# Memory layer of a hybrid model: recalls by head pairs on block-diagonal memories, values subtracted on GpSimd, recalled values turned by transposes

## The reference, cut to what matters

```python
def step(carry, inp):
    mem, z = carry
    q_s, k_s, v_s, qn_s, kn_s = inp
    scores = jnp.einsum('bhnd,bhmd->bhnm', q_s, k_s) * SCALE
    sdpa = jnp.einsum('bhnm,bhmd->bhnd', softmax(where(mask, scores, -inf)), v_s)
    sq, sk = elu1(qn_s), elu1(kn_s)
    num, den = sq @ mem, (sq @ z)[..., None]
    out = beta * num / (den + 1e-06) + (1.0 - beta) * sdpa
    prev_v = (sk @ mem) / (sk @ z)[..., None]
    mem = mem + sk.T @ (v_s - prev_v)
    z = z + sk.sum(axis=2)
    return (mem, z), out
```

## Time and profile before

| what | value |
|---|---|
| median of the runs | 2560.41 us |
| span of the profiled execution | 2623.8 us |
| instructions in it | 79243 |
| TensorE matmul busy | 2176.9 us (83%) |
| VectorE busy | 1700.0 us (65%) |
| ScalarE busy | 1437.8 us (55%) |
| GpSimd busy | 1106.7 us (42%) |
| memory layer, first instruction to the last addition to x | 1729 to 2450 us |

### The profile page before, as it was taken

One profiled execution on the slowest core, in us unless ns is written; L12 is line 12 of the kernel. 1 busy time (PEld: TensorE's weight loads), 2 busy tenths in 40 slices (PEclk: granted clock), 3 DMA queues, 4 the chain that ended last, 5 costly groups with the idle time before them and its releaser, 6 DMA issues. The chain is left out here.

```text
span 2623.8 us, 79243 instructions
## 1 busy us (share of the span) xinstructions
PE 2176.9 (83%) x30448; PEld 1549.2 (59%) x30448; DVE 1700.0 (65%) x5819; ACT 1437.8 (55%) x3704; POOL 1106.7 (42%) x1076
## 2 busy tenths in 40 slices
PE   6499948589964889899999977948999999999696
PEld 3288845379862233333334336937778777787396
DVE  6722247642336778787878833358999989899522
ACT  5455544355552256455455555537777767776353
POOL 2066644146654120120200004547777777776164
PEclk7699979789986799998989888969999999999798
DMA  4011120011125121111111000121111111111013
GB/s 133 33 42 43 43 85 2 33 32 44 43 93 163 55 58 31 38 39 31 35 46 35 5 33 29 41 85 54 54 53 56 52 53 55 52 56 52 35 42 92
DMA packets 76025, 134.96 MB, mean 51 GB/s; under 512 B 17225, under 2 KB 32264, under 8 KB 73224
## 3 DMA queue, kind: packets, MB, share of 16 engines
q1 hardware_dynamic: 62080, 102.07, 12.6%
q0 software_dynamic: 13568, 27.81, 3.7%
q10 hardware_dynamic: 8, 0.00, 0.0%
HBM read 65.19 MB, written 32.79 MB: 37 GB/s over the span
## 5 line engine op out<-in xcount | busy, mean ns | idle before, releaser
L1544 ACT ACTIVATE ca_pt<-ca_ps 128x512 f32<-128x512 f32 (+3 forms) x768 | 341.1, 491 | 322.3 <-PE ca_ps L1649 137.2
L734 PE MATMUL ffn_ps<-ffn_xst,ffn_up_w 128*128 128x128 f32 x3392 | 420.8, 278 | 0.2 <-issue 0.2
L734 PEld LDWEIGHTS ffn_ps<-ffn_xst,ffn_up_w 128*128 128x128 f32 x3392 | 402.9, 195 | 1.2 <-issue 1.2
L857 DVE TENSOR_TENSOR ffn_hid<-ffn_sg,ffn_ps 128x512 f32<-128x512 f32 x212 | 145.8, 688 | 359.2 <-PE ffn_ps L734 110.9
L576 POOL DMA_INDIRECT ffn_xs<-ffn_x,ffn_token_at x212 | 205.2, 968 | 301.5 <-DVE ffn_token_at L840 165.5
L581 POOL DMA_INDIRECT ffn_y<-ffn_ys,ffn_result_at x212 | 208.8, 985 | 139.2 <-DVE ffn_ys L863 82.3
L1645 PE MATMUL ca_ps<-ca_stacks 75*128 75x512 bf16 (+3 forms) x768 | 245.2, 342 | 18.3 <-ACT ca_pt L1544 10.7
L1777 DVE TENSOR_REDUCE ca_m_far<-ca_ps 128x1 f32<-128x128 f32 (+5 forms) x384 | 236.7, 616 | 30.3 <-PE ca_ps L1623 27.9
L643 ACT ACTIVATE ffn_sg<-ffn_ps 128x512 f32<-128x512 f32 x212 | 125.7, 593 | 233.6 <-remote 182.3
L1623 PE MATMUL ca_ps<-ca_stacks 72*128 72x512 bf16 (+3 forms) x768 | 223.4, 356 | 34.1 <-DVE ca_m_near L1778 21.9
L1778 DVE CUSTOM_DVE_ANT_0 ca_spill<-ca_ps,ca_bias_q 128x256 f32<-128x256 f32 (+1 forms) x512 | 201.1, 397 | 10.9 <-PE ca_ps L1623 10.9
(11 more groups left out here) (340 smaller groups left out, 4742.0 us busy)
## 6 DMA issues: line engine op xcount, KB each, us to landing
im_mates<-im_t SPq DMA_DIRECT2D x256, 128.0 KB
ffn_got<-ffn_y SPq DMA_DIRECT2D x48, 256.0 KB, 5.8
ca_stacks<-scratch_q_piece SPq DMA_DIRECT2D x16, 576.0 KB
ca_stacks<-scratch_k_piece SPq DMA_DIRECT2D x48, 192.0 KB
ffn_x<-ffn_xn SPq DMA_DIRECT2D x32, 256.0 KB, 2.0
w_w<-in_L_ffn_experts_w_dram SPq DMA_DIRECT2D x2, 2048.0 KB, 12.0
ffn_xs<-ffn_x,ffn_token_at POOLq DMA_INDIRECT x212
ffn_y<-ffn_ys,ffn_result_at POOLq DMA_INDIRECT x212
```

What stands on the lines that cost most here:

```text
L734: last = nc.tensor.matmul(ps[:, bank, j * P:j * P + P], up_w[:, n % WS, first + j * P:first + j * P + P], xst[:, n % 2, :], start=True, st ...
L1544: nc.scalar.activation(pt[:, i % 8, lo - c0:hi - c0], ps[:, tile_bank(i), lo - c0:hi - c0], ACT.Exp, scale=SCALE).then_inc(p_ready, 1)
```

## The change

1. A second copy of the memories, `mem_by`, holds for each of the two heads of a pair a block of 65 columns, with that head's memory on its own half of the partitions and zeros on the other. SyncE fills it: at slot k, behind the two DMAs for `mates`, it waits for `mem_ready` of step k - 4 and sends the two halves of that step's memory, two DMAs of 64 partitions with 520 float32 each.
2. `prev` and `num` run over pairs: 8 float32 matmuls each, of a 128x32 stationary piece on 130 columns of `mem_by`. All of `prev` is in bank 0 and all of `num` in bank 1. `prev` waits for those DMAs (`placed`) in place of `mem_ready`.
3. VectorE forms the recalled value times the reciprocal of all four heads by one instruction (`known`), and GpSimd subtracts the values (`surprise`), between `spread` and `rotate` of its slot.
4. The recalled values are turned by `transpose` in place of the matmul with the identity.
5. GpSimd sets `mem_by` ahead of the loops, 4160 columns on 128 partitions and twice 32 columns on 64, and TensorE and VectorE wait for that too.

```diff
+        mem_by = s.sb("mem_by", [P, NQ, 2, BATCH, PB, E1])
...
-        prev_view, num_view = (both_banks(c, PB * E1).rearrange("p e (k d) -> p e k d", k=PB) for c in (PR, NU))
+        prev_view, num_view = (ps[:, bank, 0:QH * E1].rearrange("p (h d) -> p h d", d=E1) for bank in range(2))
...
                     for odd in range(2):
                         sp.dma_start(mates[1 - odd:P:2, k % 2, :], t2[odd:P:2, k % 2, :]).then_inc(mates_ready[k % 2], 16)
+                    if 0 <= k - 4 < N - NQ:
+                        j = k - 4
+                        sp.wait_ge(S["mem_ready"], j + 1)
+                        for e in range(2):
+                            half = slice(D * e, D * e + D)
+                            sp.dma_start(mem_by[half, j % NQ, e], mem[half, j % NQ]).then_inc(placed[j % NQ], 16)
...
                 pool.wait_ge(S["made"], 13)
+                nc.gpsimd.memset(mem_by[:], 0.0).then_inc(S["made"], 1)
+                pool.wait_ge(S["made"], 14)
+                for e in range(2):
+                    nc.gpsimd.memset(mem_by[D * e:D * e + D, :, e, :, :, D:E1], 1.0e-6).then_inc(S["made"], 1)
+                pool.wait_ge(S["made"], 16)
...
+                def surprise(j):
+                    pool.wait_ge(S["known"], j + 1)
+                    pool.wait_ge(S["lifted"], j + 1)
+                    new = uu[:, j % 2, :, 0:D]
+                    nc.gpsimd.tensor_tensor(new, new, values_of(j), ALU.subtract).then_inc(S["u_ready"], 1)
...
                     if 0 <= k - 3 < N:
                         spread(k - 3)
+                    if 0 <= k - 3 < LEARNED:
+                        surprise(k - 3)
                     if k < N:
                         rotate(k)
...
+                def for_pairs(fn):
+                    for blk in range(PB):
+                        for b in range(BATCH):
+                            last = fn(blk, b, slice(SEG * b, SEG * b + SEG))
+                    return last
...
-                        nc.tensor.matmul(ps[:, UP + n, OT:OT + P], m1[:, j % 2, 2 * n:2 * n + 2, :].rearrange("p h d -> p (h d)"), g.ident[:], start=True, stop=False, skip_group_check=True)
+                        nc.tensor.transpose(ps[:, UP + n, OT:OT + P], m1[:, j % 2, 2 * n:2 * n + 2, :].rearrange("p h d -> p (h d)"), g.ident[:])
...
-                        pe.wait_ge(S["mem_ready"], j - NQ + 1)
-                    for_heads(lambda half, bank, blk, b, tok: nc.tensor.matmul(ps[tok, bank, PR + blk * E1:PR + blk * E1 + E1], el[half, r, PB + blk, tok], mem[half, q, b, blk, :],
+                        pe.wait_ge(placed[q], 32 * (j // NQ))
+                    for_pairs(lambda blk, b, tok: nc.tensor.matmul(ps[tok, 0, blk * 2 * E1:blk * 2 * E1 + 2 * E1], el[:, r, PB + blk, tok], mem_by[:, q, :, b, blk, :],
...
-                    for h in range(QH):
-                        e, n = h // PB, h % PB
-                        last = nc.vector.scalar_tensor_tensor(uu[:, r, h, 0:D], prev_view[:, e, n, 0:D], rd[:, h:h + 1], values_of(j)[:, 2 * n + e, :], ALU.mult, ALU.subtract)
-                    last.then_inc(S["u_ready"], 1)
+                    nc.vector.tensor_tensor(uu[:, r, :, 0:D], prev_view[:, :, 0:D], bl(rd[:], D), ALU.mult).then_inc(S["known"], 1)
```

More of the change, by code:

```diff
@@ L1856, in memory_layer @@
     E1 = D + 1
-    PR, NU, SC = 0, PB * E1, 2 * PB * E1
+    SC = 2 * PB * E1
     UP, OT = 4, 192
@@ L1899, in memory_layer @@
                  "ab_used", "below_ready", "er_ready", "below_exp", "el_ready", "rope_ready", "lift_ready", "lifted", "scored", "recalled", "s1_ready", "rd_ready", "nm_ready",
-                 "u_ready", "den_ready", "dn_ready", "m1_ready", "p_ready", "share_ready", "own_gated", "rsum_ready", "pn_ready", "pt_ready", "pte_ready",
-                 "upd_ready", "mem_ready", "weighed", "ot_copied", "out_ready", "x_ready", "stats")
+                 "known", "u_ready", "den_ready", "dn_ready", "m1_ready", "p_ready", "share_ready", "own_gated", "rsum_ready", "pn_ready", "pt_ready", "pte_ready",
+                 "upd_ready", "mem_ready", "placed_a", "placed_b", "placed_c", "placed_d", "weighed", "ot_copied", "out_ready", "x_ready", "stats")
         S = {n: s.sem(n) for n in names}
         mates_ready = (S["mates_even"], S["mates_odd"])
+        placed = (S["placed_a"], S["placed_b"], S["placed_c"], S["placed_d"])
         def both_banks(first, width):
@@ L2113, in prev @@
                     if j >= NQ:
-                        pe.wait_ge(S["mem_ready"], j - NQ + 1)
-                    for_heads(lambda half, bank, blk, b, tok: nc.tensor.matmul(ps[tok, bank, PR + blk * E1:PR + blk * E1 + E1], el[half, r, PB + blk, tok], mem[half, q, b, blk, :],
-                                                                               start=True, stop=True, skip_group_check=True))
+                        pe.wait_ge(placed[q], 32 * (j // NQ))
+                    for_pairs(lambda blk, b, tok: nc.tensor.matmul(ps[tok, 0, blk * 2 * E1:blk * 2 * E1 + 2 * E1], el[:, r, PB + blk, tok], mem_by[:, q, :, b, blk, :],
+                                                                   start=True, stop=True, skip_group_check=True))
                 def num(j):
                     q, r = j % NQ, j % 3
-                    for_heads(lambda half, bank, blk, b, tok: nc.tensor.matmul(ps[tok, bank, NU + blk * E1:NU + blk * E1 + E1], el[half, r, blk, tok], mem[half, q, b, blk, :],
-                                                                               start=True, stop=True, skip_group_check=True)).then_inc(S["recalled"], 1)
+                    for_pairs(lambda blk, b, tok: nc.tensor.matmul(ps[tok, 1, blk * 2 * E1:blk * 2 * E1 + 2 * E1], el[:, r, blk, tok], mem_by[:, q, :, b, blk, :],
+                                                                   start=True, stop=True, skip_group_check=True)).then_inc(S["recalled"], 1)
                 def lift_values(k):
@@ L2167, in learn @@
                                 tok = slice(SEG * b, SEG * b + SEG)
-                                last = nc.tensor.matmul(b_up[half, b, blk * E1:blk * E1 + E1], keys[tok, blk, half], uu[tok, r, PB * parity + blk, :],
+                                last = nc.tensor.matmul(b_up[half, b, blk * E1:blk * E1 + E1], keys[tok, blk, half], uu[tok, r, 2 * blk + parity, :],
                                                         start=True, stop=True, skip_group_check=True)
@@ L2176, in lift_keys @@
                     last.then_inc(S["lift_ready"], 1)
-                pe.wait_ge(S["made"], 13)
+                pe.wait_ge(S["made"], 16)
                 for c in range(2 * BATCH):
@@ L2217, in _ @@
                 dve.wait_ge(S["g_ready"], 1)
-                dve.wait_ge(S["made"], 13)
+                dve.wait_ge(S["made"], 16)
                 nc.vector.tensor_scalar_add(gate[:, 1:3, :], gate[:, 1:3, :], 1.0).then_inc(S["setup"], 1)
@@ L2260, in recall @@
                                                    ALU.mult, ALU.add).then_inc(S["s1_ready"], 1)
-                    nc.vector.reciprocal(rd[:].rearrange("p (e k) -> p e k", e=2), prev_view[:, :, :, D]).then_inc(S["rd_ready"], 1)
+                    nc.vector.reciprocal(rd[:], prev_view[:, :, D]).then_inc(S["rd_ready"], 1)
                     dve.wait_ge(S["s1_ready"], j + 1)
@@ L2264, in recall @@
                     dve.wait_ge(S["rd_ready"], j + 1)
-                    nc.vector.scalar_tensor_tensor(dn[:].rearrange("p (e k) -> p e k", e=2), num_view[:, :, :, D], 1.0e-6,
-                                                   gate[:, 1, q * QH:q * QH + QH].rearrange("p (k e) -> p e k", e=2), ALU.add, ALU.mult).then_inc(S["den_ready"], 1)
-                    dve.wait_ge(S["lifted"], j + 1)
+                    nc.vector.scalar_tensor_tensor(dn[:], num_view[:, :, D], 1.0e-6, gate[:, 1, q * QH:q * QH + QH], ALU.add, ALU.mult).then_inc(S["den_ready"], 1)
                     if 2 <= j < LEARNED:
                         dve.wait_ge(S["upd_ready"], j - 1)
-                    for h in range(QH):
-                        e, n = h // PB, h % PB
-                        last = nc.vector.scalar_tensor_tensor(uu[:, r, h, 0:D], prev_view[:, e, n, 0:D], rd[:, h:h + 1], values_of(j)[:, 2 * n + e, :], ALU.mult, ALU.subtract)
-                    last.then_inc(S["u_ready"], 1)
+                    nc.vector.tensor_tensor(uu[:, r, :, 0:D], prev_view[:, :, 0:D], bl(rd[:], D), ALU.mult).then_inc(S["known"], 1)
                     dve.wait_ge(S["den_ready"], j + 1)
@@ L2278, in recall @@
                         dve.wait_ge(S["weighed"], j - 1)
-                    nc.vector.tensor_tensor(sorted_heads(m1[:, r]), num_view[:, :, :, 0:D], over(dn[:], D), ALU.mult).then_inc(S["m1_ready"], 1)
+                    nc.vector.tensor_tensor(m1[:, r], num_view[:, :, 0:D], bl(dn[:], D), ALU.mult).then_inc(S["m1_ready"], 1)
                 def add(p):
```

## The result

The changed kernel takes 2567.14 us (median of 20 runs) against 2559.05; the ratio is 1.0037, 95% interval 1.0023 to 1.0052. It is slower, by 8.1 us, a little less than half of the 17.6 us forecast. The profiled execution spans 2564.0 us, but that of before 2623.8, so the two are compared by layer and not by span.

The account below looks back on a forecast made before the run. A circle of waits between VectorE and TensorE was taken to bound each slot; a new one of 5.26 us plus 0.15 against 5.31 gave +12.4 us, memset +4.2, rounded up to +17.6: 2578 us, range 2548 to 2610.

Parts of the forecast that it names:

- a new circle through `spread`, the subtraction and `learn`: From remember over turn_p, spread, GpSimd's subtraction and learn back to remember: 5.26 us a slot, replacing the old circle's 5.11.
- Disturbances: Late partner DMAs and features holding up L2248 add 0.15 us a slot, with 0.07 and 0.35 as bounds.
- The end: Last two tiles, where TensorE has twice the output products and no room: total rounded up from +16.6 to +17.6 us.
- The circle's length: Sum of the waits and operations around the new circle: 5.26 us, between 5.20 and 5.33, with 0.61 for the subtraction.
- Recalls, transposes, placing: In each slot: recalls by pairs take 0.59 us, two transposes save 0.17 us on TensorE, placing DMAs cost nothing.
- Ahead of the loops: GpSimd's memset of 4160 columns and two small ones, all on the path since TensorE waits for them: +4.2 us.
- Rival 2: At L2155, learn meets its operand in time and TensorE's slot of 5.0 us decides: faster, 2539 us, chance 0.14.
- Rivals 3 and 4: 3: later DMAs, 0.35 us a slot, 2602 us, chance 0.12; 4: column groups do not overlap, +370 us, chance 0.02.
- Rival 1: Same circle, but late partner DMAs cost 0.07 us a slot, covered by GpSimd's new work: 2567 us, chance 0.34.

Follow-up runs that it names:

- `light_behind`: Kernel before with one-instruction multiplication on VectorE, GpSimd's subtraction behind spread and transposes, recalls single, no second copy; ratio 1.0068 to the kernel before.
- `vector_subtracts`: Changed kernel with the subtraction back on VectorE in four instructions; ratio 1.0008 to the kernel before.
- `doubled`: Changed kernel with one more GpSimd operation of 128x256 between spread and the subtraction, result unused; 2695.64 us against 2601.27 of the kernel before on that chip.
- `sub_first`: Changed kernel with GpSimd's subtraction ahead of spread instead of behind it; ratio 0.9942 to the kernel before.
- `light`: Kernel before with one-instruction multiplication on VectorE, GpSimd's subtraction ahead of spread and transposes, recalls single, no second copy; ratio 0.9935 to the kernel before.

## Why the prediction was right in sign and too large in size

- *Sign and mechanism.* Right: the main forecast, slower by a new circle through `spread`, the subtraction and `learn`. Moving it away, lengthening it and rebuilding it without the pairs all moved the time as the circle says.
- *The sum.* Forecast were +12.4 us in the slots, +4.2 ahead of the loops and +1.0 at the end; the traces have +8.5, +3.5 and -4.1. Two terms failed: the disturbances of a slot and the end.
- *Disturbances, the first step that failed.* I took 0.15 us a slot on top of the circle; it is 0.08, about 8 us less in all. Two smaller errors hid most of this in the slots' sum: the circle is 0.05 us longer than forecast, about 6 us, and the mean slot of before, which I read as 5.31 from the middle of the layer, is 5.33 over all of it, about 2 us. `light_behind` shows that 0.15 would have been near for single recalls (0.18). GpSimd waited for partner DMAs in 52 slots before, 50.5 us. With single recalls and the subtraction's cover, in `light_behind`, it is 19 slots and 17.6 us. What I did not see is that the kernels with recalls by pairs are disturbed less besides: 16 slots and 10.2 us in the changed kernel, and 27.2 us without the cover, in `vector_subtracts`. Why is open.
- *The end, the second step that failed.* I added 1 us for the last tiles, since TensorE has twice the output products there; the trace has -4.1 us. I had read only the middle of the layer, where `learn` bounds. At the end it does not exist, and the shorter recall and a clock that did not fall come out as a gain. Of the three parts of the sum this one missed by most, 5.1 us, and a part of it may be chance, as said above.
- *The circle's length.* 5.26 us forecast, 5.30 to 5.31 measured. The term at fault is the subtraction: 0.61 by L1989, 0.68 in fact. L1989 reads broadcast operands; `doubled`'s added operation of the same size, which does not, took 0.73. Half of `spread`'s 1.27 us would have said 0.64.
- *Recalls, transposes, placing.* Recalls by pairs 0.58 (0.59). The two transposes took 0.38 us against 0.61, a little better than L2175 promised. Placing nothing, as forecast.
- *Ahead of the loops.* +4.2 forecast, +4.0 to TensorE's start, +3.5 to the first sines.
- *Rivals.* Rival 2 named the right place, L2155: in `sub_first`, where the way from `turn_p` to `learn` no longer holds the subtraction, TensorE's own slot decides with 5.07 us (5.08 by the forecast's sum). Rivals 3 and 4 fell. Rival 1, 2567 us from disturbances of 0.07, has the measured time and the measured size of the disturbances, although I gave the forecast more. That its time is met to the microsecond is in part luck: its slot of 5.33 us is 0.06 too short, and the end that it leaves out gives most of that back.

## What to carry to other kernels

Work that is moved to an idle engine lands in a queue. Ask what stands in front of it there, and how much earlier its reader used to get its operand. Here 0.68 us of work behind `spread` made a clean slot 5.30 us long instead of 5.11; with the same work ahead of `spread` it is 5.07. Read the first and last turns of a loop too, since another chain can bound them.

## What was not expected

- TensorE, padded to the old number of instructions while the doubled DMA traffic runs, stood still for up to 1.98 us (PEld at L2144) in the loops, with no wait in the profile. The kernel before, with as many instructions and without that traffic, showed at most 1.1 us at L2115, but `light`, also without it, once showed 1.90 us (PEld at L2123). So the traffic is not shown to be the cause, and what TensorE lacks there is open.
- A memset on GpSimd, which reads nothing, took VectorE's normalisation from 2.14 to 4.10 us. The first of the eight operations lasted 2.50 us and ended 0.08 us behind the memset. The kernel before has the same beside its memset of 1.83 us, a group of 3.21 us, which I had not read. The Trainium skill, SBUF — State Buffer, section Who interferes with whom, says that single-source operations such as this one can use both port pairs and are then shut out by a GpSimd operation as a whole; this agrees. The multiplication of two operands in SBUF had shown a like meeting before, 293 ns against up to 545.
